# First batch on eight PSUM banks, early loads over two queues, first head group's q/k copied inside SBUF

## The chip, the cores and the metric

The kernel runs on one core of a Trainium2 chip. The metric is the device time of one execution in microseconds. Engines are named as in the profile: PE (TensorE), with PEld for its weight loads, DVE (VectorE), ACT (ScalarE), POOL (GpSimd) and SP (SyncE, which only issues DMAs). SPq and POOLq are their queues.

## The reference

Input x is (4, 512, 256), 4 batches of 512 tokens. All is fp32.

```
qh = heads((layernorm(x) @ wq + bq)) * gqw      # gqw, gkw: one weight per token
gq = sum over tokens of qh
gk = sum over tokens of (heads(ctx @ wk + bk) * gq * gkw)
out = heads(ctx @ wv + bv) * gk + qh
x1 = x + tanh(g_xattn) * (out @ wo + bo)
src = layernorm(x1)
attn = softmax(q k^T / 4) v  with q, k, v = src @ Wq + Bq, ... in 16 heads of 16
z = layernorm(src + attn @ Wo + Bo)
expert = floor(z @ router_w + router_b) mod 4
out = x1 + tanh(g_ffn) * layernorm(z + relu(z @ W1[expert] + b1) @ W2[expert] + b2)
```

## The kernel before

Each batch goes through the same stages. "x" are the layernorm statistics, "scale" normalises, cT and xT transpose ctx and x on PE, gv computes the gate vectors gq and gk from the token sums, Q and V are the gated projections, Y is the output projection; then "x1" (statistics), "src" (the second layernorm, L628), sT (its transpose), the projections q, k and v of the attention, and O after it. A task of PE such as q has two indices (halves of the features) and two halves (the two parts of the contraction).

The projections q and k are kept as a high and a low part for the fp32r products: ACT writes the high part (`HL[:, j, 0, :]`, L541), DVE the rest (L633). For a head group g the products need three pieces of q under each other (high, low, high) in QS and three of k (high, high, low) in KS, per half c of the heads. They get there through memory: `store_qk` (L291) writes HL to `qk_dram`, `load_stack` (L303, L306) reads twelve pieces of 16 partitions by two head pairs. A group has 16 row maxima (PE L818 into the three amax banks, DVE L686); they are negated, split and transposed, and go through `m_dram` (L312, L315) into rows 48 and 49 of QS, where the score product (L827, units u = 0 to 255) takes them up. ACT takes the exponentials (L549), PE multiplies by v (L839).

From u = -54 on all engines walk the same tables by unit (BLOCKS for PE, EVICT for ACT, VECTOR for DVE, QUEUE for SP, GPSIMD for POOL); batch b's entries are shifted by 64 b units, so batch 1's first part lies among batch 0's maxima, which run 24 units ahead of the scores. Each engine executes its list in order and waits on semaphores.

Batch 0 goes ahead of the tables, in the order of `LEAD` (L248). All side work uses two PSUM banks (`side`); the other six stand unused until the maxima start. SP's order ahead of the tables (L318 to L349) is: x and ctx of batch 0, the gates and gqw as a column, two rows broadcast to all partitions, five bias columns (element by element), eight broadcast rows, all weights, x and ctx of batch 1 (which wait for the first batch's x1 to be stored), and then the stores and stacks of batch 0. DVE computes twelve constants once all those loads have landed (L701 to L717), and PE's gv waits for all twelve. POOL computes the reciprocal roots (L396, L398), adds biases to xin (L413, L421), stores x1 (L423), adds a bias to src, stores it (L431) and reads it back into t_r (L437) after the store has landed; its list is in order as well.

## Time and profile before

| | us |
|---|---|
| median of 3 runs | 615.15 (612.97 to 615.59) |
| the profiled execution | 614.73 |
| its span | 612.9 |
| PE busy | 491.3 (80%) |
| DVE busy | 390.2 (64%) |
| ACT busy | 244.7 (40%) |
| POOL busy | 207.1 (34%) |
| mean granted TensorE clock | 0.858 of full |

Shares of the span are means over stages of different kinds. The first scores come at 112.2 us and the last at 417.3 us of the span; ahead of them lies the first batch's preparation, behind them the routed feed-forward.

### The profile page before, as it was taken

To read this page: it belongs to the slowest core of one execution; us is meant where nothing else is said; L and a number is where in the kernel's file an instruction comes from. 1 tells how busy PE (TensorE), PEld (TensorE's weight loads), DVE (VectorE), ACT (ScalarE), POOL (GpSimd) and SP (SyncE) were. 2 spreads that over 40 slices of the span, in tenths; PEclk is the share of its full clock that TensorE was granted. 3 is DMA by queue.
4 is the path that set the end of the run, shared out by engine and by line. 5 is a ranking of instruction groups with operands and counts; after the bars stand their busy time and mean duration, and the time that the engine had idled before them with its cause. 6 is when DMAs were issued, how large, how long until landed. Compare 5 with 4: busy or idle time off the path is not lost. (4 is left out here: it accounts for less than half of the span.)

```text
span 612.9 us, 8282 instructions
## 1 busy us (share of the span) xinstructions
PE 491.3 (80%) x2528; PEld 281.8 (46%) x2528; DVE 390.2 (64%) x871; ACT 244.7 (40%) x482; POOL 207.1 (34%) x273
## 2 busy tenths in 40 slices
PE   2095769899898999999979798887239998988970
PEld 2053343434423433434332242223239988888970
DVE  2333446988768889679976779703885655655552
ACT  2000200465435456244654546447005555454440
POOL 3115110141101323403303248522144565455552
PEclk9997957999789899799995879655659999899995
DMA  5701844055334353632665840020021122111220
GB/s 145 164 0 38 282 129 67 3 198 180 84 78 121 114 196 93 139 102 58 152 187 140 176 112 3 2 70 1 1 68 35 51 61 58 45 52 40 64 54 25
DMA packets 41795, 55.00 MB, mean 90 GB/s; under 512 B 14367, under 2 KB 26143, under 8 KB 41760
## 3 DMA queue, kind: packets, MB, share of 16 engines
q1 hardware_dynamic: 36432, 38.84, 24.3%
q0 software_dynamic: 5328, 15.74, 8.5%
q8 instruction: 16, 0.26, 0.2%
q14 instruction: 19, 0.16, 0.1%
HBM read 37.51 MB, written 17.83 MB: 90 GB/s over the span
## 5 line engine op out<-in xcount | busy, mean ns | idle before, releaser
L549 ACT ACTIVATE probs<-sc 128x512 f32<-128x512 f32 x256 | 141.2, 595 | 178.0 <-PE sc L827 175.5
L686 DVE TENSOR_REDUCE mx<-amax 128x1 f32<-128x512 f32 x256 | 166.6, 677 | 58.9 <-PE amax L818 58.8
L827 PE MATMUL sc<-QS,KS 50*128 50x512 f32 x256 | 111.7, 520 | 15.3 <-ACT probs L549 12.2
L818 PE MATMUL amax<-KS,QS 48*128 48x512 f32 x256 | 110.4, 515 | 14.4 <-DMA KS<-qk_dram 8.5
L827 PEld LDWEIGHTS sc<-QS,KS 50*128 50x128 f32 x256 | 45.6, 210 | 121.2 <-issue 64.9
L818 PEld LDWEIGHTS amax<-KS,QS 48*128 48x128 f32 x256 | 43.9, 205 | 32.0 <-DVE mx L686 15.2
L1174 PE MATMUL amax<-W_hi,hid_hi 128*128 128x256 f32 x160 | 48.2, 301 | 3.8 <-DVE hid_lo L1074 3.6
L1174 PE MATMUL amax<-W_hi,hid_lo 128*128 128x256 f32 x160 | 46.6, 291 | 0.0
L1174 PE MATMUL amax<-W_lo,hid_hi 128*128 128x256 f32 x160 | 46.6, 291 | 0.0
L495 POOL TENSOR_TENSOR an<-av,rec 128x256 f32<-128x256 f32 x16 | 10.2, 637 | 106.8 <-DVE rec L675 106.7
L839 PE MATMUL pv<-probs,V1b 128*32 128x512 f32 x256 | 44.1, 769 | 1.4 <-ACT probs L549 1.2
L396 POOL TENSOR_SCALAR var_eps<-mv 128x4 f32<-128x4 f32 x12 | 2.8, 235 | 120.5 <-DVE mv L571 116.1
L758 PE MATMUL side<-xcT,w_first 128*128 128x512 f32 x64 | 40.8, 760 | 0.0
L839 PE MATMUL pv<-probs,V1a 128*32 128x512 f32 x256 | 39.6, 695 | 0.0
L991 ACT ACTIVATE t_a<-sc,b_col 128x256 f32<-128x256 f32 x40 | 19.3, 482 | 42.6 <-PE sc L1164 42.4
L930 POOL DMA_INDIRECT out_dram<-slot_z,ids_now x22 | 24.2, 1099 | 35.4 <-DVE slot_z L1114 32.0
L758 PE MATMUL side<-srcT,w_second 128*128 128x512 f32 x64 | 34.6, 667 | 0.8 <-ACT srcT L535 0.8
L1174 PEld LDWEIGHTS amax<-W_hi,hid_hi 128*128 128x128 f32 x160 | 32.0, 200 | 6.2 <-DVE hid_lo L1074 6.0
L1164 PE MATMUL sc<-slot_xT,W_hi 128*128 128x256 f32 x160 | 31.5, 292 | 1.5 <-DVE slot_xT L1068 1.5
L1174 PEld LDWEIGHTS amax<-W_lo,hid_hi 128*128 128x128 f32 x160 | 32.1, 200 | 0.0
L1174 PEld LDWEIGHTS amax<-W_hi,hid_lo 128*128 128x128 f32 x160 | 32.0, 200 | 0.0
L1074 DVE TENSOR_TENSOR hid_lo<-t_a,hid_hi 128x512 fp32r<-128x512 f32 x40 | 27.0, 690 | 6.0 <-ACT hid_hi L992 5.7
(180 smaller groups left out, 865.8 us busy)
## 6 DMA issues: line engine op xcount, KB each, us to landing
qk_dram<-HL SPq DMA_DIRECT2D x16, 512.0 KB, 4.6
QS<-qk_dram SPq DMA_DIRECT2D x96, 64.0 KB, 2.9
KS<-qk_dram SPq DMA_DIRECT2D x96, 64.0 KB, 3.0
W_sb<-in_L_ffn_W SPq DMA_DIRECT2D x8, 512.0 KB, 5.5
xc<-in_x SPq DMA_DIRECT2D x4, 512.0 KB, 3.6
xc<-in_ctx SPq DMA_DIRECT2D x4, 512.0 KB, 4.8
x_dram<-xc POOLq DMA_DIRECT2D x4, 512.0 KB, 3.4
res_dram<-t_a POOLq DMA_DIRECT2D x4, 512.0 KB, 5.4
```

The source lines that it names most:

```text
L495: nc.gpsimd.tensor_tensor(an[:, :, g % 2, :], av_v[:, :, 0:DH], rec[:, :].unsqueeze(2).broadcast_to([P, S // 32, DH]), ALU.mult).then_inc( ...
L549: nc.scalar.activation(probs[:, n % 8, c * 512:(c + 1) * 512], sc[c][:, :], ACT.Exp, scale=SCALE).then_inc(exp_done, 1)
L686: nc.vector.reduce_max(mx[:, to:to + 1], amax[m % 3][:, :], AX.X).then_inc(max_done, 1)
L758: last = nc.tensor.matmul(bank[:, :], w[:, k, c * P:(c + 1) * P], src[:, k, :], start=(k == 0), stop=(k == KD - 1))
L818: nc.tensor.matmul(amax[m % 3][:, :], QS[rows, pair, chunk * P:(chunk + 1) * P], KS[rows, pair, :], start=True, stop=True).then_inc(A_full, 1)
L827: nc.tensor.matmul(sc[c][:, :], KS[rows, pair, kc * P:(kc + 1) * P], QS[rows, pair, :], start=True, stop=True).then_inc(sc_full, 1)
L839: last = nc.tensor.matmul(pv[32 * hh:32 * hh + 32, :], V1[b % 2][:, kc, 8 * c + pair, :], probs[:, (2 * r + hh // 2) % 8, c * 512:(c + 1) ...
L930: nc.gpsimd.indirect_dma_start(out_rows, bass.IndirectOffsetOnAxis(ap=ids_now[:, a:a + 1], axis=0), slot_z[:, a, :], None, bounds_check=NT ...
L991: nc.scalar.activation(hid[:, q % 2, f % 2, :], hid_bank[f % 4], ACT.Relu, bias=bias)
L1074: nc.vector.tensor_tensor(low, hid[:, q % 2, :, :], high.bitcast(fp32), ALU.subtract).then_inc(hid_split, 1)
L1164: last = nc.tensor.matmul(hid_bank[f % 4], w, slot_xT[:, xp, k, :], start=((k, (xp, wp)) == steps[0]), stop=((k, (xp, wp)) == steps[-1]))
L1174: last = nc.tensor.matmul(amax[a][:, 0:D], (hid_hi, hid_lo)[xp][:, f, a * P:(a + 1) * P], w, start=(f == 0 and (xp, wp) == PARTS[0]), stop ...
```

## The change

- Side work of batch 0 uses eight banks: `LEAD_BANK` gives each task its own, `bank_of` replaces `side_bank`. The order is cT, V0, xT, V1, gv, Q, Y, .... In all batches V's eviction (L612) now comes ahead of Q's (L607) and goes straight into oT; in later batches they change places in the tables.
- The two transposes of t_a wait tile by tile instead of for all four tiles.
- gqw and the five bias vectors are loaded as 14 rows of 128 by ACT's queue, transposed in one PE instruction ahead of everything and copied by ACT into `columns`. ACT's queue loads wv as well. On SP, x and ctx are followed by the two broadcast rows, wk, wq, wo, the gates, and the other rows and weights; each weight has its own semaphore.
- DVE's constants are in three parts: six ahead of the ctx sums, bo's row behind them, five between Q and Y. tanh moves on ACT behind xT. V1's fills move behind the second layernorm. POOL's x1 step waits until all of src is scaled.
- Three products whose result is not used stand on PE ahead of sT.
- For the first head group of batch 0, q and k go from HL to QS and KS by DMAs inside SBUF, 16 partitions each: SP issues q of the first pair, then x of batch 1, then k of both pairs; ACT issues q of the second pair. The stores to memory follow, for groups 1 to 3. ctx of batch 1 is loaded ahead of them.
- In later batches group 0's q half of the stack is asked for at -36 and its k half at -31; group 2's at -6 instead of -10.

The core of the diff (indented less):

```
 pv = psum("pv", [P, 512])
+BANKS = side + sc + amax + [pv]
...
-         -31: ("stack", 0), -22: ("stack", 1), -10: ("stack", 2), 2: ("stack", 3)}
+QUEUE = {-117: ("load", 0), -42: ("store", 0), -39: ("store", 1), -37: ("store", 2), -36: ("stack", (0, "q")), -34: ("store", 3),
+         -31: ("stack", (0, "k")), -22: ("stack", (1,)), -6: ("stack", (2,)), 2: ("stack", (3,))}
 QUEUE.update({16 * g - 8: ("maxima", g) for g in range(G)})
...
-FIRST_PART = [("cT", 0), ("cT", 1), ("xT", 0), ("xT", 1), ("gv", 0), ("Q", 0), ("V", 0), ("Q", 1), ("V", 1), ("Y", 0), ("Y", 1)]
-LEAD = FIRST_PART + [("sT", 0), ("sT", 1), ("q", 0), ("q", 1), ("k", 0), ("k", 1), ("v", 0), ("v", 1)]
+LEAD = [("cT", 0), ("cT", 1), ("V", 0), ("xT", 0), ("xT", 1), ("V", 1), ("gv", 0), ("Q", 0), ("Q", 1), ("Y", 0), ("Y", 1),
+        ("sT", 0), ("sT", 1), ("q", 0), ("q", 1), ("k", 0), ("k", 1), ("v", 0), ("v", 1)]
+LEAD_BANK = {"cT": (0, 1), "V": (4, 5), "xT": (2, 3), "gv": (6,), "Q": (7, 0), "Y": (1, 2),
...
-def side_bank(task, i):
-
-    return 1 if task in ("gv", "V") else 0 if task == "Q" else i % 2
+def bank_of(task, i, b):
+
+    if b == 0 and task in LEAD_BANK:
+        return LEAD_BANK[task][i]
+    return 1 if task in ("gv", "Q") else 0 if task == "V" else i % 2
...
+        for i, part in enumerate(((0, 1, 0), (0, 0, 1))[side_of == "k"]):
+            at = 64 * c + DH * i
+            sp.dma_start(to[at:at + DH, r, :].bitcast(fp32), HL[DH * r:DH * r + DH, c + 2 * (side_of == "k"), part, :].bitcast(fp32)).then_inc((stack_loaded[0], stack_rest)[r], 16)
+
     def load_stack(b, g, sides="qk"):
         if g == 0:
-            for j in range(2 if sides == "q" else 4):
+            for j in range(4)[2 * (sides == "k"):4 - 2 * (sides == "q")]:
                 sp.wait_ge(qk_stored[j], b * 16 + 16)
+        elif b == 0:
+            for j in range(4):
+                sp.wait_ge(qk_stored[j], 16)
         wait(sp, sc_full, (b - 1) * UNITS + 16 * (g + 1))
         for c in range(2):
...
-    load_batch(0)
-    sp.dma_start(gqw_col[:, :], gqw.rearrange("(t p) o -> p (t o)", p=P), allow_slow_non_contiguous=True).then_inc(gates_loaded, 16)
+    load_tokens(0)
+    load_context(0)
+    sp.dma_start(gkw_row[:, :], gkw.rearrange("s o -> (s o)").partition_broadcast(P)).then_inc(rows_s_loaded, 16)
+    sp.dma_start(t1[:, :], gqw.rearrange("s o -> (s o)").partition_broadcast(P)).then_inc(rows_s_loaded, 16)
+    load_weight("wk", wk, wk_loaded)
+    load_weight("wq", wq, wq_loaded)
+    load_weight("wo", wo, wo_loaded)
     sp.dma_start(gates[:, 0:1], g_xattn.partition_broadcast(P)).then_inc(gates_loaded, 16)
     sp.dma_start(gates[:, 1:2], g_ffn.partition_broadcast(P)).then_inc(gates_loaded, 16)
-    sp.dma_start(t1[:, :], gqw.rearrange("s o -> (s o)").partition_broadcast(P)).then_inc(w_loaded, 16)
-    sp.dma_start(gkw_row[:, :], gkw.rearrange("s o -> (s o)").partition_broadcast(P)).then_inc(w_loaded, 16)
-    for i, v in enumerate((bq, bk, bv, Bq, Bk)):
-        sp.dma_start(cols[:, i, :], v.rearrange("(k p) -> p k", p=P), allow_slow_non_contiguous=True).then_inc(w_loaded, 16)
-    for i, v in enumerate((bo, Bo, Bv, ln1_g, ln1_b, router_w.rearrange("d o -> (d o)"), ln2_g, ln2_b)):
-        sp.dma_start(rows_bc[:, i, :], v.partition_broadcast(P)).then_inc(w_loaded, 16)
-    sp.dma_start(rb_col[:, :], router_b.partition_broadcast(P)).then_inc(w_loaded, 16)
-    for n, ap in (("wq", wq), ("wk", wk), ("wv", wv), ("wo", wo)):
...
+    sp.dma_start(rb_col[:, :], router_b.partition_broadcast(P)).then_inc(rows_loaded, 16)
     for n, ap in (("Wq", Wq), ("Wk", Wk), ("Wv", Wv)):
         load_weight(n, ap, W_loaded)
...
                 sp.dma_start(w_sb["Wo"][r:r + DH, t, :], Wo[h * DH:(h + 1) * DH, :]).then_inc(W_loaded, 16)
-    load_batch(1)
-    for side_of, js in (("q", (0, 1)), ("k", (2, 3))):
-        for j in js:
-            store_qk(0, j)
-
-        sp.wait_ge(stack_ready, 1)
-        load_stack(0, 0, side_of)
+    load_context(1)
+    sp.wait_ge(lo_done, 1)
+    sp.wait_ge(stack_ready, 1)
+    load_parts("q", 0, 0)
+    sp.wait_ge(lo_done, 2)
+    load_parts("q", 1, 0)
+    load_tokens(1)
+    for r in range(2):
+        for c in range(2):
+            sp.wait_ge(lo_done, 3 + c)
+            load_parts("k", c, r)
+    for j in range(4):
+        store_qk(0, j)
     for g in range(1, G):
         load_stack(0, g)
...
-            pool.wait_ge(consts_ready, CONSTS)
+            pool.wait_ge(bo_ready, 1)
         for t in range(TT):
...
     def store_x1(b):
+        if b == 0:
+            pool.wait_ge(consts_ready, CONSTS)
...
 def act_program(act):
-    act.wait_ge(gates_loaded, 48)
-    nc.scalar.activation(tg[:, :], gates[:, :], ACT.Tanh).then_inc(gates_ready, 1)
+    for v, first in ((gqw.rearrange("s o -> (s o)"), 0), (bq, 4), (bk, 6), (bv, 8), (Bq, 10), (Bk, 12)):
+        n = v.shape[0] // P
+        act.dma_start(column_rows[first:first + n, :], v.rearrange("(k p) -> k p", p=P)).then_inc(columns_loaded, 16)
+    act.dma_start(w_sb["wv"][:, :, :], wv.rearrange("(k p) n -> p k n", p=P)).then_inc(wv_loaded, 16)
+    act.wait_ge(columns_full, 1)
+    nc.scalar.activation(columns[:, :], amax[2][:, 0:14], ACT.Identity).then_inc(columns_done, 1)
...
             wait(act, qk_stored[j], b * 16)
+            if b == 1:
+                act.wait_ge(stack_loaded[0], 12 * 16)
+                act.wait_ge(stack_rest, 6 * 16)
...
     for task, i in LEAD:
         side_work(task, i, 0)
+        if (task, i) == ("xT", 1):
+            act.wait_ge(gates_loaded, 32)
+            nc.scalar.activation(tg[:, :], gates[:, :], ACT.Tanh).then_inc(gates_ready, 1)
+    act.wait_ge(lo_done, 2)
+    act.wait_ge(stack_ready, 1)
+    for c in range(2):
+        for i, part in enumerate((0, 1, 0)):
+            row = 64 * c + DH * i
+            act.dma_start(QS[row:row + DH, 1, :].bitcast(fp32), HL[DH:2 * DH, c, part, :].bitcast(fp32)).then_inc(q_rest, 16)
...
             nc.vector.tensor_tensor(gkb[:, :], gk[:, :], cols[:, 2, :], ALU.mult).then_inc(gk_done, 1)
+        elif task == "V":
+
+            dve.wait_ge(V_full, b * 2 + i + 1)
+            dve.wait_ge(gk_done, b * 2 + 2)
+            wait(dve, Y_full, b * 2)
+            nc.vector.scalar_tensor_tensor(oT[:, i, :], bank[:, :], gk[:, i:i + 1], C1[:, i, :], ALU.mult, ALU.add).then_inc(t1_done, 1)
         elif task == "Q":
             dve.wait_ge(Q_full, b * 2 + i + 1)
-            dve.wait_ge(gk_done, b * 2 + 2)
-            wait(dve, csum_done, b * 2 + 2)
...
-
-            dve.wait_ge(V_full, b * 2 + i + 1)
...
-            nc.vector.scalar_tensor_tensor(oT[:, i, :], bank[:, :], gk[:, i:i + 1], t1[:, :], ALU.mult, ALU.add).then_inc(o_done, 1)
+            nc.vector.scalar_tensor_tensor(oT[:, i, :], bank[:, :], gkb[:, i:i + 1], oT[:, i, :], ALU.add, ALU.add).then_inc(o_done, 1)
...
             if i == 0:
-                dve.wait_ge(o_done, min(b + 3, B) * 2)
+                dve.wait_ge(csum_done, min(b + 3, B) * 2)
+                dve.wait_ge(consts_ready, CONSTS)
                 wait(dve, dot_done, b * (TT + 2))
...
         side_work("scale", t, 0)
-    dve.wait_ge(w_loaded, W_LOADS * 16)
-    dve.wait_ge(gates_ready, 1)
-
-    for row, g in ((BO, 0), (G2, 1), (B2, 1)):
-        nc.vector.tensor_scalar(rows_bc[:, row, :], rows_bc[:, row, :], tg[:, g:g + 1], None, ALU.mult).then_inc(consts_ready, 1)
+    dve.wait_ge(rows_s_loaded, 32)
+    dve.wait_ge(columns_done, 1)
...
-    nc.vector.tensor_tensor(rows_bc[:, GRW, :], rows_bc[:, G1, :], rows_bc[:, RW, :], ALU.mult).then_inc(consts_ready, 1)
-    dve.wait_ge(consts_ready, 8)
...
-                side_work("src", t, 0)
+
+    def later_constants():
+        dve.wait_ge(rows_loaded, 8 * 16)
+        for row in (G2, B2):
+            nc.vector.tensor_scalar(rows_bc[:, row, :], rows_bc[:, row, :], tg[:, 1:2], None, ALU.mult).then_inc(consts_ready, 1)
+        nc.vector.tensor_tensor(rows_bc[:, GRW, :], rows_bc[:, G1, :], rows_bc[:, RW, :], ALU.mult).then_inc(consts_ready, 1)
+        dve.wait_ge(consts_ready, EARLY_CONSTS + 3)
+        nc.vector.reduce_sum(gsum[:, 2:3], rows_bc[:, GRW, :], AX.X).then_inc(consts_ready, 1)
+        dve.wait_ge(csum_done, 2)
+        nc.vector.tensor_tensor_reduce(out=t1[:, 0:D], in0=rows_bc[:, B1, :], in1=rows_bc[:, RW, :], scale=1.0, scalar=rb_col[:, 0:1],
+                                       op0=ALU.mult, op1=ALU.add, accum_out=gsum[:, 3:4]).then_inc(consts_ready, 1)
+
+    side_work("cT", 0, 0)
+    side_work("cT", 1, 0)
+    dve.wait_ge(gates_ready, 1)
+    dve.wait_ge(bo_loaded, 16)
+    nc.vector.tensor_scalar(rows_bc[:, BO, :], rows_bc[:, BO, :], tg[:, 0:1], None, ALU.mult).then_inc(bo_ready, 1)
+    for task, i in (("gv", 0), ("V", 0), ("V", 1), ("Q", 0), ("Q", 1)):
+        side_work(task, i, 0)
+    later_constants()
+    side_work("Y", 0, 0)
+    for t in range(2):
+        side_work("x1", t, 0)
+    side_work("Y", 1, 0)
+    for t in range(2, TT + 1):
+        side_work("x1", t, 0)
+    for t in range(TT):
+        side_work("src", t, 0)
+    for v in V1:
+        nc.vector.memset(v[:, :, :, DH:2 * DH], 1.0).then_inc(v1_ready, 1)
+    for task, i in LEAD[LEAD.index(("q", 0)):]:
+        side_work(task, i, 0)
     for u in range(BEGIN, END + OVER):
         if 0 <= u + AHEAD < END:
...
-    def transposes(bank, src, c, full):
+    last_use = [None] * len(BANKS)
+
+    def transposes(bank, src, c, full, ready=None, b=0):
         for t in range(TT):
+            if ready is not None and c == 0:
...
             pe.wait_ge(stack_loaded[g % G], g // G * 192 + 192)
+        if m == 8:
+            pe.wait_ge(stack_rest, 6 * 16)
+            pe.wait_ge(q_rest, 6 * 16)
...
     pe.wait_ge(pool_ready, 3)
+    pe.wait_ge(columns_loaded, 6 * 16)
+    nc.tensor.transpose(amax[2][:, 0:14], column_rows, ident[0:14, 0:14]).then_inc(columns_full, 1)
     for task, i in LEAD:
-        if task == "gv":
-            pe.wait_ge(consts_ready, CONSTS)
+        for first, s, count in ((("V", 0), wv_loaded, 16), (("V", 0), cT_done, 2), (("gv", 0), wk_loaded, 16), (("gv", 0), wq_loaded, 16), (("Y", 0), wo_loaded, 16), (("sT", 0), W_loaded, W_LOADS2 * 16)):
+            if (task, i) == first:
+                pe.wait_ge(s, count)
+        if (task, i) == ("gv", 0):
+            pe.wait_ge(columns_done, 1)
         if (task, i) == ("sT", 0):
-            pe.wait_ge(W_loaded, W_LOADS2 * 16)
+            for _ in range(3):
+                nc.tensor.matmul(amax[2][:, :], w_sb["wq"][:, 0, 0:P], cT[:, 0, :], start=True, stop=True)
         for half in range(1 if task in ("cT", "xT", "gv", "sT") else 2):
             side_work(task, i, half, 0)
+    for n in range(len(side), len(BANKS)):
+        pe.wait_ge(*last_use[n])
     pe.wait_ge(stack_ready, 1)
     pe.wait_ge(v1_ready, 2)
...
```

## Rows read from the trace of the kernel before

**Rows 1.** Six stretches: length, busy time (and instructions) per engine, granted clock, DMA share, GB/s.
```profile
0.00:28.00 28.00, 3.88 (x16) 3.14 (x16) 6.59 (x22) 3.84 (x8) 5.67 (x11) 1.00 0.70 167
28.00:62.00 34.00, 23.11 (x62) 13.78 (x63) 13.22 (x31) 1.88 (x3) 12.41 (x16) 0.87 0.08 23
62.00:82.30 20.30, 11.24 (x40) 6.54 (x38) 7.46 (x18) 3.95 (x7) 5.00 (x8) 0.84 0.74 241
82.30:112.20 29.90, 28.36 (x74) 13.47 (x74) 20.39 (x39) 0.69 (x2) 0.00 (x0) 0.69 0.39 76
112.20:417.80 305.60, 280.87 (x1293) 109.22 (x1292) 231.13 (x492) 154.07 (x284) 91.05 (x116) 0.87 0.41 111
417.80:612.90 195.10, 143.82 (x1050) 135.67 (x1048) 111.39 (x271) 80.28 (x178) 92.95 (x122) 0.85 0.15 44
```

**Rows 2.** Timeline, 0 to 31 us: start, duration, engine, line, operation, count, [idle before <-releaser].
```profile
5.91 1.94 PE L753 MATMUL side<-ident,xc 128*128 128x128 f32 x8 [5.91 <-DMA xc<-in_ctx]
...
10.81 0.20 POOL L406 TENSOR_TENSOR rg<-rstd,gqw_col 128x4 f32<-128x4 f32 x1
...
24.54 0.88 DVE L705 TENSOR_SCALAR rows_bc<-rows_bc,tg 128x256 f32<-128x256 f32 x3 [12.11 <-DMA w_first<-in_L_xattn_wo]
...
29.72 0.98 DVE L591 CUSTOM_DVE_ANT_0 t<-xcT,gkw_row 128x512 f32<-128x512 f32 x1
```

**Rows 3.** Timeline, 30 to 62 us.
```profile
30.85 1.84 PE L790 MATMUL side<-xsum,w_first 128*128 128x1 f32 x8 [16.34 <-DVE csum L591]
...
34.26 9.57 PE L758 MATMUL side<-xcT,w_first 128*128 128x512 f32 x16
...
44.77 3.69 PE L766 MATMUL side<-w_first,oC 128*128 128x256 f32 x16 [0.94 <-DVE oC L612]
...
48.49 0.75 DVE L618 SCALAR_TENSOR_TENSOR xc<-side,tg,xc 128x512 f32<-128x512 f32 x1 [0.98 <-PE side L766]
...
52.45 2.19 DVE L628 TENSOR_SCALAR t_a<-xc,mv,rstd 128x256 f32<-128x256 f32 x4 [1.48 <-POOL rstd L398]
...
57.26 2.76 POOL L429 TENSOR_TENSOR t_a<-t_a,rows_bc 128x256 f32<-128x256 f32 x4
...
57.50 5.46 PE L758 MATMUL side<-srcT,w_second 128*128 128x512 f32 x6 [0.78 <-ACT srcT L535]
```

**Rows 4.** Timeline, 62 to 82.5 us.
```profile
62.02 0.75 DVE L633 SCALAR_TENSOR_TENSOR HL<-side,cols,HL 128x512 fp32r<-128x512 f32 x1 [7.38 <-ACT HL L541]
...
67.20 0.76 POOL L437 DMA_DIRECT2D t_r<-res_dram  x1 [6.06 <-DMA res_dram<-t_a]
...
76.81 1.08 PE L753 MATMUL side<-ident,t_a 128*128 128x128 f32 x4 [4.30 <-DVE t_a L585]
...
80.50 0.42 SPq L303 DMA_DIRECT2D QS<-qk_dram  x1
...
82.34 0.79 PE L818 MATMUL amax<-KS,QS 48*128 48x512 f32 x2 [4.45 <-DMA KS<-qk_dram]
```

**Rows 5.** Timeline, 97 to 116 us.
```profile
97.56 0.42 SPq L306 DMA_DIRECT2D KS<-qk_dram  x1
...
102.70 1.98 PE L758 MATMUL side<-xcT,w_first 128*128 128x512 f32 x4
...
105.14 0.67 SPq L312 DMA_DIRECT2D m_dram<-mT  x1
...
112.18 0.50 PE L827 MATMUL sc<-QS,KS 50*128 50x512 f32 x1
```

**Rows 6.** DMA issues, 0 to 100 us: KB each, median us from issue to landing.
```profile
qk_dram<-HL SPq DMA_DIRECT2D x4, 512.0 KB, 4.5
QS<-qk_dram SPq DMA_DIRECT2D x24, 64.0 KB, 2.9
...
gqw_col<-in_L_xattn_gqw SPq DMA_DIRECT2D x1, 2.0 KB, 4.5
...
w_first<-in_L_xattn_wv SPq DMA_DIRECT2D x1, 256.0 KB, 8.9
```

78 lines of the change are left out of this document (37 added, 41 removed), and 2 rows, old and new, of the table BLOCKS.

## The prediction

> **What bounds the kernel now.** I read the profile in three steps: the busy time cut by stretches, then the timeline of the first 116 us, then the landing times of the DMAs. The stretches [rows 1] show a kernel of three parts. From 112.2 to 417.8 us runs the attention loop (305.6 us, TensorE busy in 280.9 of them), from 417.8 to 612.9 the routed feed-forward, 195.1 us. The rest, 112.2 us, is the lead-in: batch 0 goes through its first part, its q/k/v and its first head group's maxima before the first score. In 0 to 28 us TensorE is busy for 3.9 us, DVE for 6.6. The loop and the tail start when the lead-in ends, and no line of the tail is touched, so nearly the whole question is by how much the first score, at 112.18 [rows 5], comes earlier.
>
> The lead-in is a chain with four links. (1) DVE's constants start at 24.54, released by the last weight load after 12.11 us of idling, and TensorE's first real block (gv) starts at 30.85 behind them [rows 2, 3]. (2) gv 3.7 us (twice 1.84), Q and V 9.57, Y 3.69, the second layernorm, and the q block starts at 57.50 [rows 3]. (3) The low half of q0 is done at 62.77, is stored and read back, and the first product for the maxima runs at 82.34, released by a DMA into KS [rows 4]. (4) The maxima, with batch 1's first part between them, take from 82.34 to 105.14, the way of the maxima through memory until the first score 7.04 more [rows 5].
>
> **The change, part by part.** I keep a clock for the new kernel and compare at each mark.
>
> *Loads.* SP issues x and ctx first as now. The ACT queue issues six loads of rows (14 rows of 128 numbers) and wv. Seven issues at about 0.47 (as the stack loads: 36 from 80.50 to 97.56 [rows 4, 5]) put wv out at some 4 us. Landing of the small ones is bounded by 2.9 us (a 64 KB stack load) and 4.5 us (gqw_col) [rows 6]: 7 to 8.5 us on the clock, I take 7. wv is bounded by 2.9 below and 8.9 above, its present landing behind the full queue [rows 6]: 7 to 13 us; the stretch 62 to 82.3 moves 241 GB/s against 167 in the first 28 [rows 1], so without the element-wise column loads ahead of it I take the lower half, under 10. The new wait of TensorE on the columns stands ahead of the ctx transposes, which now start at 5.91 [rows 2]: they slip to 7.3 (1.94 us, ACT's copies until 9.8), and everything of PE is queued behind. The rule of the Trainium skill that speaks against this part is in "DMA: Bandwidth & Descriptors", section "Issuing engines are not separate DMA queues": transfers started by scalar, sync or gpsimd run on the same 16 engines, and a second issuer saves only issue time. By it the second queue would be worth seven issues of 0.47, 3.3 us of SP's time, and no bandwidth. No row of before has an ACT-issued load, so it isn't shown here.
>
> *First part.* V0 runs as soon as ctx is transposed and wv is there: 9.9. Q and V took 9.57 for 16 records [rows 3], V0 as a quarter at the cold rate is 3.4 (5.46 for 6 records is 0.91 each, 1.98 for 4 is 0.5 [rows 3, 5]). The x transposes follow at 13.3 (x is scaled by then: rg is there at 10.81 even now [rows 2]), V1 to about 18.3, gv to 21 (3.7 cold, 2 warm; I take 2.7), Q0 and Q1 to 24.4 at the warm rate. DVE's constants for this part (two sums, two C1, two bG) lie beside V0 and the x transposes. Its csum pass needs 0.98 at most each [rows 2], done by 14. From gv on DVE does V0, V1, Q0, Q1 at 0.75 each; the last waits for Q1: o is done at 25.2. Y 3.69 on PE to 29.0, DVE's last Y step at 29.0, which is at 48.49 now [rows 3]: minus 19.5. The five later constants (some 2 us) stand between Q and Y on DVE, beside Y's first half (1.85); uncovered they cost 2. The eight banks remove the waits of V on Q's eviction; within Q and V these are small, as 16 records fill the 9.57 without a gap [rows 3]; I give them nothing.
>
> *Second layernorm to q.* From 48.49 to the scaling at 52.45 is 3.96 us, unchanged. The scaling takes 2.19 for four now because POOL adds beside it; the new wait on src_done takes POOL away, and the transposes follow tile by tile. I take 1.4 and 0.6 us of overlap. The wait delays POOL's four adds (2.76 as their like [rows 3]) by 1 us, for which only the store of x1 waits. DVE's two fills of V1, now beside gv, go behind the scaling, where DVE has nothing before q's low half. Three products on no one's data fill 6 records before sT: 2.6 us warm, done at 31.6, ahead of the first scaled tile at 32.9; cold they would end at 34.1 and cost 1. Their purpose can be priced from rows: the 6 cold records of q cost 5.46 where warm ones cost 3, and the stretch 28 to 62 has a mean granted clock of 0.87 [rows 1, 3]. The page "TensorE: Matmul & The Clock Gate", section "The HAM clock gate", of the Trainium skill says that the slow level is the default and activity releases it, so filling is the right cure; by it the gain is these 2.5 us. The q block starts at 35.4 instead of 57.50, q0's low half is done at 38.7 instead of 62.77: minus 24. At the warm rate (1.7 a task) k1's low half is done at 43.8 and v at 45.9.
>
> *First group without memory.* Now: store (4.5), wait, six loads, landing 2.9, for q and again for k [rows 6]. New: q pieces at 38.8 to 42, then x of batch 1, k pieces of the first pair until 45.3 (three issues of 0.47 for each half), landing 2.9: the stacks stand at 48.2. That is 34 us before 82.34. But I don't grant it all, for batch 1's x transpose is ahead of the first maxima in TensorE's order (76.81 and 82.34 now [rows 4]). POOL has to finish batch 0's residual: adds until 41.5, its store, and 6.06 us of waiting for it before it may reload [rows 4]: 48.3, then 0.76 for the issue, then batch 1's scale (1.48 from statistics to scaling [rows 3] and 0.20 for rg [rows 2], with the hand-over some 1.8), DVE's scaling 1.4, the transpose behind its first tile: 51 to 52.3. So the first maxima start at 52.0, bounded by 48.2 and by 54 (a slower reload): minus 30.3.
>
> *Maxima to first score.* Now 29.84 us from 82.34 to 112.18 [rows 4, 5], at a mean clock of 0.69, DVE busy 20.4 [rows 1]. At the same pace the first score comes at 81.9. At the full clock the stretch can't be shorter than DVE's 20.4; but another queue then binds. SP has the four stores (48.0 to 50), waits for their landing (4.5 alone, 6 for 2 MB together: 56), and issues 36 stack loads, 17.5 us [rows 4, 5]: 73.5. Only then does it take the first maxima, after which 7.04 us pass: 80.5. Both bounds are so close that I take 81.0: minus 31.2. The six ACT-issued pieces of the second pair lie in ACT's idle time (43 to 46 us; its next job is a copy at 47.5).
>
> *Loop.* Later batches change V and Q places (the same records), ask for three more landings long past, and issue q's half of the stack before k is stored: 6 issues less, 2.8 us, where PE waits for KS; between nothing and 2 us in each of two batches. The second group's loads move by four steps, still ahead of use. I take 0 and keep minus 4 in the range.
>
> Sum against the profiled execution, 614.73 us (span 612.9, 1.83 around it): 614.7 - 31.2 = 583.5. It lies 0.4 below the median of 615.15, which gives 584; for the many marks at which something may slip I go 1 up: 585.
>
> **The rivals.**
>
> *A: the early loads stay the limit* (0.2). For it: 4.7 MB come in by 28 us (167 GB/s times 28 [rows 1]), nearly all of it is still loaded, and wv, wk and wq share engines with two 256 KB broadcasts. Against: the low rate falls into the column loads. If weights land 6 us later than I think, gv starts at 24 and the gain is 25: 590; range 588 to 597.
>
> *B: the loop gains too* (0.17). The clock stays high between v and the maxima, q's earlier stack loads save 2 us a batch, and the loop's mean of 0.87 rises. Gain 36 to 42: 573 to 579. Against: SP's 36 loads bind at 80.5 whatever the clock.
>
> *C: the direct move does not reach the first product, or is slow* (0.08). A piece has 16 partitions with 2 KB each; if 18 of them take the 4.5 us of a 512 KB store one after the other, the first maxima start at 55 to 58 and the score at 86: 588 to 591. In its weak form the move does not do what it says because the x transpose at 50.9 is later than the stack; that is in my forecast.
>
> *D: slower than before* (0.02). The mechanism: loop and tail at a lower granted clock. The loop's 280.9 us of TensorE at 0.87 [rows 1] grow to 326 at 0.75, +45 against -31: 629. It decides from a mean of 0.78 on (280.9 x 0.87/0.78 = 313, +32). For it only that the clock is 0.69 in one stretch; against it that the loop's order is unchanged.
>
> **How the numbers follow.** Forecast with its own range 580 to 588: 0.53; A 0.2, B 0.17, C 0.08, D 0.02. The range 576 to 595 leaves out the end of B, the end of A and D, some 0.15. A change of less than 0.5% is about what a measurement of this kernel can't tell from none; only D and a failure of every part lie there or above. Faster 0.97, same 0.01, slower 0.02.
>
> **What would show it.** gv at 18 to 19 instead of 30.85; last Y step on DVE near 29; q block near 35.4 with a granted clock of 1.0; stacks landed before batch 1's x transpose, which is near 51 and releases the first maxima; SP issuing stack loads until about 73; first score at 80 to 82; loop 304 to 307 us and tail 195. It is wrong if the first maxima come before 48 or after 56, if the first score is not within 78 to 86, or if the loop's length moves by over 4 us.

## The result, and the profile after

| | before | after |
|---|---|---|
| median, us | 614.06 (609.24 to 615.59, 4 runs) | 583.08 (573.46 to 589.22, 4 runs) |
| the profiled execution | 614.73 | 580.17 |
| its span | 612.9 | 578.1 |
| first score / last score | 112.2 / 417.3 | 83.1 / 382.8 |

The ratio of the two medians is 0.950. A ratio with an interval, here 0.941 (0.928 to 0.954), counts for each kernel only the runs within 1.5% of its fastest, which leaves out the longer two of after's four (585.98 and 589.22); a kernel with only one such run is given none. In the last row stand three parts: the lead-in went from 112.2 to 83.1 us (-29.1), the loop from 305.1 to 299.7 (-5.4), the tail from 195.6 to 195.3.

The lead-in is the way to the first score, the loop lies between the first and the last score, and the tail behind them. The stretches after, cut at the first maxima and at the first score (length, busy us and instructions of PE, PEld, DVE, ACT, POOL, granted clock, DMA share, GB/s), against [rows 1]:

```profile
0.00:28.00 28.00, 18.06 (x67) 11.35 (x68) 14.85 (x40) 4.02 (x9) 8.44 (x15) 1.00 0.70 178
28.00:52.45 24.45, 16.46 (x57) 9.17 (x55) 11.93 (x31) 5.03 (x8) 11.24 (x17) 0.92 0.51 157
52.45:83.07 30.62, 28.98 (x74) 14.62 (x73) 20.61 (x39) 1.38 (x4) 2.85 (x4) 0.67 0.54 125
83.10:382.80 299.70, 274.77 (x1291) 107.82 (x1290) 232.00 (x491) 154.27 (x284) 91.14 (x116) 0.89 0.43 113
382.80:578.10 195.30, 144.21 (x1054) 135.78 (x1050) 111.56 (x271) 80.19 (x178) 93.76 (x122) 0.85 0.15 43
```

In its first 28 us PE works 18.1 instead of 3.9, with DMA at the same share (0.70) and much the same rate (178 against 167 GB/s). The DMA engines carry hardly more than before; what changed is which load stands first and who waits for which. The loop's row has 274.8 us of PE at 0.89 where it had 280.4 at 0.87.

Timeline of the first part (start, duration, engine, line, operation, count, idle before and its releaser), against [rows 2, 3]:

```profile
8.22 0.25 PE L910 MATMUL amax<-ident,probs 14*128 14x14 f32 x1 [8.22 <-DMA probs<-in_L_ffn_bk]
...
11.12 0.50 PEld L821 LDWEIGHTS amax<-xcT,w_first 128*128 128x128 f32 x2 [1.15 <-DMA w_first<-in_L_xattn_wv]
11.15 3.65 PE L821 MATMUL amax<-xcT,w_first 128*128 128x512 f32 x4 [0.78 <-ACT xcT L567]
...
12.85 0.69 DVE L641 CUSTOM_DVE_ANT_0 t<-xcT,gkw_row 128x512 f32<-128x512 f32 x1 [0.15 <-DVE bG L759]
...
17.23 0.95 PE L853 MATMUL amax<-xsum,w_first 128*128 128x1 f32 x8
...
27.28 0.75 DVE L667 SCALAR_TENSOR_TENSOR xc<-sc,tg,xc 128x512 f32<-128x512 f32 x1 [0.19 <-PE sc L829]
```

PE's first block waits for the columns (8.22; their rows lie in a buffer that the profile calls probs), V0's weight load for wv (1.15 us of idling), V0's first product for ACT's copy of the ctx transposes, done at 11.00. The two came close together: wv had landed at about 10.6 (issued at 2.85, 7.7 us to landing). gv starts at 17.23 instead of 30.85. Its two records take 0.95 and 1.03 us, and DVE's last Y step is at 27.28 instead of 48.49. A block is called warm below when its products run at the pace of a clock granted in full, and cold at the pace of half of it. V0 is cold by its own duration, four products in 3.65 us where V1's four take 1.88 (from 15.51), though the row of the first 28 us shows a granted clock of 1.00.

Two things had to be there for gv: the weights and the sums of the tokens. Before, wk was issued at 14.00 and took 8.6 us to land:

```profile
14.00 0.47 SPq L274 DMA_DIRECT2D w_first<-in_L_xattn_wk  x1
```

```profile
w_first<-in_L_xattn_wk SPq DMA_DIRECT2D x1, 256.0 KB, 8.6
```

So before's gv could not have started ahead of about 22.6 whatever DVE did (an estimate, 14.00 + 8.6). In fact it waited for DVE, which idled 12.11 us for the last of the loads, then computed constants from 24.54 on, and began its pass over ctx for the sums (csum, L591) only at 28.88. After, wk is issued at 2.82 and takes 8.1, and that pass (L641) starts at 12.85. By this estimate at least 5 of gv's 13.6 us come from wk landing earlier, that is from the order of the loads and from the columns that stood ahead of them, and at most 8 from the shorter waits for constants. No run parts the two. From here to the first maxima, against [rows 3, 4]:

```profile
33.74 3.67 PE L821 MATMUL amax<-srcT,w_second 128*128 128x512 f32 x8 [0.83 <-ACT srcT L570]
...
36.46 0.75 DVE L682 SCALAR_TENSOR_TENSOR HL<-amax,columns,HL 128x512 fp32r<-128x512 f32 x1 [2.22 <-ACT HL L580]
...
41.11 0.91 SPq L288 DMA_DIRECT2D xc<-in_x  x1
...
42.06 7.50 SPq L309 DMA_DIRECT2D KS<-HL  x12
...
43.58 0.76 POOL L469 DMA_DIRECT2D t_r<-res_dram  x1 [3.24 <-DMA res_dram<-t_a]
...
47.03 1.40 DVE L615 BATCH_NORM_STATS2 stats<-xc 128x6 f32<-128x256 f32 x4 [2.00 <-DMA xc<-in_x]
...
51.17 1.35 PE L816 MATMUL side<-ident,t_a 128*128 128x128 f32 x4 [5.42 <-DVE t_a L633]
...
52.45 0.79 PE L883 MATMUL amax<-KS,QS 48*128 48x512 f32 x2
```

The eight products of the q block take 3.67 us with the clock granted in full; six took 5.46 before. Batch 1's x is issued at 41.11 behind q's pieces, is in use at 47.03, and its scaled tile releases the transpose (51.17) right behind which the maxima start at 52.45, against 82.34. No wait for a KS piece is shown ahead of it. The end of the lead-in, against [rows 4, 5]:

```profile
73.92 0.42 SPq L327 DMA_DIRECT2D KS<-qk_dram  x1
74.39 0.67 SPq L333 DMA_DIRECT2D m_dram<-mT  x1
...
77.62 1.28 SPq L336 DMA_DIRECT2D QS<-m_dram  x2
...
79.53 3.61 PE L829 MATMUL side<-w_first,oC 128*128 128x256 f32 x8
...
83.07 0.49 PE L892 MATMUL sc<-QS,KS 50*128 50x512 f32 x1
```

And four DMA issues (KB each, median us from issue to landing), against [rows 6]:

```profile
KS<-HL SPq DMA_DIRECT2D x12, 32.0 KB, 3.9
...
w_first<-in_L_xattn_wv ACTq DMA_DIRECT2D x1, 256.0 KB, 7.7
...
QS<-HL SPq DMA_DIRECT2D x6, 32.0 KB, 2.0
QS<-HL ACTq DMA_DIRECT2D x6, 32.0 KB, 4.4
```

### The profile page after: what moved, and what is told of

It is laid out like the page before. It is cut to its first block and busy times, and to the rows that moved or that the text cites. A ratio compares the mean times of both kernels' runs of the same rounds, so it can differ in the third digit from the quotient of the medians.

```text
span 578.1 us, 8313 instructions
## 1 busy us (share of the span) xinstructions
PE 482.5 (83%) x2535; PEld 278.8 (48%) x2535; DVE 390.9 (68%) x871; ACT 244.9 (42%) x483; POOL 207.4 (36%) x273
## 5 line engine op out<-in xcount | busy, mean ns | idle before, releaser
L892 PE MATMUL sc<-QS,KS 50*128 50x512 f32 x256 | 108.1, 502 | 14.9 <-ACT probs L588 12.5
L883 PE MATMUL amax<-KS,QS 48*128 48x512 f32 x256 | 106.9, 500 | 11.0 <-DMA KS<-qk_dram 6.2
L892 PEld LDWEIGHTS sc<-QS,KS 50*128 50x128 f32 x256 | 43.7, 202 | 115.9 <-ACT probs L588 56.1
L883 PEld LDWEIGHTS amax<-KS,QS 48*128 48x128 f32 x256 | 42.0, 197 | 28.0 <-DVE mx L736 13.8
L904 PE MATMUL pv<-probs,V1a 128*32 128x512 f32 x256 | 35.4, 626 | 0.1
L821 PE MATMUL side<-xcT,w_first 128*128 128x512 f32 x52 | 31.6, 715 | 0.0
L722 DVE STREAM_TRANSPOSE av<-pv 128x512 f32<-128x512 f32 x16 | 11.3, 707 | 24.8 <-PE pv L904 24.8
```

What stands on the lines that cost most here:

```text
L821: last = nc.tensor.matmul(bank[:, :], w[:, k, c * P:(c + 1) * P], src[:, k, :], start=(k == 0), stop=(k == KD - 1))
L883: nc.tensor.matmul(amax[m % 3][:, :], QS[rows, pair, chunk * P:(chunk + 1) * P], KS[rows, pair, :], start=True, stop=True).then_inc(A_full, 1)
L892: nc.tensor.matmul(sc[c][:, :], KS[rows, pair, kc * P:(kc + 1) * P], QS[rows, pair, :], start=True, stop=True).then_inc(sc_full, 1)
L904: last = nc.tensor.matmul(pv[32 * hh:32 * hh + 32, :], V1[b % 2][:, kc, 8 * c + pair, :], probs[:, (2 * r + hh // 2) % 8, c * 512:(c + 1) ...
```

## The experiments

The kernels fall into three groups, each timed beside its own runs of the kernel before: a1 to a4 (before 606.1 us), a5 to b2 (614.1) and b3 to c2 (611.6). Times compare within a group, ratios across them. A kernel's time came from 2 runs in the first two groups and from 6 in the last, so times are told beside the marks of the one profiled execution: "first maxima" and "first score". After has 52.45 and 83.07; its own code, run again (c0), 52.35 and 82.06, so a difference of 1 us in a mark tells nothing by itself.

### Undoing one part at a time

**a1_through_memory.** The first group goes through memory again: all four stores, then its twelve loads. ACT's six pieces go too; the rest stays.

```diff
-            load_parts("q", 0, 0) ... load_parts("k", c, r)
+            store_qk(0, 0); store_qk(0, 1); load_tokens(1); store_qk(0, 2); store_qk(0, 3)
-            for g in range(1, G):
+            for g in range(0, G):
                 load_stack(0, g)
```

> The changed kernel, but its first head group goes through memory as before (all four stores, then the twelve loads of group 0); everything else as changed. Marks of the changed kernel: first product for the maxima 52.45, first score 83.07. Theory 1 (batch 1's x chain gates the first maxima, the copies inside SBUF save only a few us): stores out by 43, landed by 48, twelve loads issued until 54 and landed at 57: first maxima at 56 to 57, first score 3 to 5 us later than 83.07 (86 to 88), since SP is free of twelve slower issues. Rival 2 (the round trip is what the change gained, as in the kernel before, where 19.6 us lay between the first low half and the first maxima): first maxima at 62 or later, first score 91 or later.

585.7 us (581.2 to 590.2). Timeline of a1:

```profile
56.58 0.79 PE L867 MATMUL amax<-KS,QS 48*128 48x512 f32 x2 [6.05 <-DMA KS<-qk_dram]
...
76.78 0.67 SPq L333 DMA_DIRECT2D m_dram<-mT  x1
```

First maxima 56.58, now released by the DMA into KS after 6.05 us; first score 86.84. The direct move is worth 4.1 us at the maxima and 3.8 at the score, of the 30 us by which the first maxima come earlier. SP had issued all loads by then and took the maxima the moment they were there (76.55 + 0.21 to 76.78); the way from maxima to score was 30.3 all the same.

**a2_no_fill.** The three products ahead of sT are taken out.

```diff
-                if (task, i) == ("sT", 0):
-                    for _ in range(3):
-                        nc.tensor.matmul(amax[2][:, :], w_sb["wq"][:, 0, 0:P], cT[:, 0, :], start=True, stop=True)
```

> The changed kernel without the three products on no one's data. TensorE then idles from 27.2 to 31.3. Theory 1: the granted clock falls to 0.5 in that gap or soon after, the first transposes and records of q run at 0.85 us instead of 0.43, q's low half comes 2 to 2.6 us later than 37.21, the first maxima 1 to 2.5 us later than 52.45. Rival 2: a gap of 4 us leaves the clock as it is, all marks within 0.3 us.

582.6 us (578.0 to 587.2). Timeline of a2:

```profile
34.20 5.96 PE L821 MATMUL amax<-srcT,w_second 128*128 128x512 f32 x8 [0.78 <-ACT srcT L570]
```

Eight records in 5.96 us instead of 3.67: +2.3, as expected. The first maxima came at 55.32, 2.9 later where 1 to 2.5 were expected, and the first score at 86.2. But the same cold block came in a6, b1 and b2, which have the fill; a6, from its timeline, and its windows (granted clock in the third column from the right; the last row is a6's loop):

```profile
34.78 5.46 PE L821 MATMUL amax<-srcT,w_second 128*128 128x512 f32 x6 [0.83 <-ACT srcT L570]
```

```profile
34.00:36.00 2.00, 1.22 (x2) 0.73 (x3) 1.12 (x2) 0.64 (x2) 2.00 (x4) 0.50 0.00 0
86.20:392.00 305.80, 281.56 (x1293) 109.31 (x1292) 232.05 (x492) 154.05 (x284) 91.13 (x116) 0.87 0.41 111
```

Of the twelve profiles with the fill (of four products in c2), after's among them, nine began the q block warm and three cold. So 2 to 3 us is what a cold block costs; how much of it the fill prevents one execution without it can't say.

**a3_two_banks.** Batch 0 uses two banks again, and the order that goes with them.

```diff
-        LEAD = [... ("V", 0), ("xT", 0), ("xT", 1), ("V", 1), ("gv", 0), ("Q", 0), ("Q", 1), ...
+        LEAD = [... ("xT", 0), ("xT", 1), ("gv", 0), ("V", 0), ("Q", 0), ("V", 1), ("Q", 1), ...
-            if b == 0 and task in LEAD_BANK:
-                return LEAD_BANK[task][i]
```

> The changed kernel with the side work of batch 0 in the two side banks again; V ahead of gv is impossible with two, so the order is cT, xT, gv, V0, Q0, V1, Q1, Y. Loads, constants, fill and copies as changed. Theory 1 (my prediction gave the banks nothing, the order with V ahead some microseconds, since V fills the wait for the loads): gv starts at about 14.5 instead of 17.23 but V and Q follow it, Q ends at 26 instead of 22.6; with bank waits between q, k and v the q block comes 3 to 4 us late and k's last low half 5 us late; first score 4 to 5 us later than 83.07. Rival 2 (the banks are a large part of the gain): first score 8 us later or more. Rival 3: under 1 us.

582.7 us, ratio 0.963 (0.952 to 0.973). Timeline of a3:

```profile
14.08 1.76 PE L851 MATMUL side<-xsum,w_first 128*128 128x1 f32 x8 [2.79 <-DVE csum L639]
...
17.40 8.89 PE L819 MATMUL side<-xcT,w_first 128*128 128x512 f32 x16
...
27.23 3.69 PE L827 MATMUL side<-w_first,oC 128*128 128x256 f32 x16 [0.94 <-DVE oC L659]
```

gv runs earlier, but 8.9 us of V and Q stand behind it, so Y starts 3.7 later than after's 23.55; first maxima 55.59, first score 86.11. The q block starts at 37.42, again 3.7 later, so two banks add nothing between Y and q. Banks and order together are worth 3 to 4 us, and it is the order that shows: V behind gv. The banks' own part is that they allow this order.

**a4_one_queue.** The seven early loads of ACT's queue go to SP, behind x and ctx.

```diff
-                act.dma_start(column_rows[first:first + n, :], ...
-            act.dma_start(w_sb["wv"][:, :, :], ...
+                sp.dma_start(column_rows[first:first + n, :], ...
+            sp.dma_start(w_sb["wv"][:, :, :], ...
```

> The changed kernel with the seven loads of ACT's queue (six of rows, wv) issued by SP right behind x and ctx; nothing else differs. Theory 1 (issuers share the engines, a second queue saves issue time only): columns are transposed at 8.2 to 9.5 (now 8.22), V0 at 11 to 12.5 (now 11.15), the SP loads behind them come 3.3 us later, the last piece of Wo is landed near 30 instead of 27, which now is a limit ahead of sT by 0.2 us only: fill and sT 1 to 2.5 us later, first score 1 to 3 us later. Rival 2 (a queue of its own brings the rows past the bulk): columns not before 11, V0 not before 14, first score 3.5 us or more later. Rival 3: no difference.

577.5 us (576.7 to 578.4), ratio 0.954 (0.944 to 0.964). First maxima 50.80, first score 80.46, 2.6 earlier than after and 1.6 earlier than c0. Its two timeline marks:

```profile
3.72 0.39 SPq L344 DMA_DIRECT2D w_first<-in_L_xattn_wv  x1
...
10.11 3.75 PE L821 MATMUL amax<-xcT,w_first 128*128 128x512 f32 x4 [0.78 <-ACT xcT L567]
```

SP issues wv 0.9 later than ACT did (2.85), and V0 still starts 1.0 earlier, and 0.6 before c0's 10.72. On SP's queue, ahead of the broadcast rows, wv took 3.5 us to land; issued by ACT beside them it took 7.7 in after and 7.7 to 9.3 in the other profiles. The expected loss of 1 to 3 us did not come, and the second queue brought nothing here. This is the side of the Trainium skill's "DMA: Bandwidth & Descriptors", section "Issuing engines are not separate DMA queues": a second issuer takes issue time off the first and adds no bandwidth. The trace agrees: with ACT as a second issuer SP's wk was out at 2.82 instead of a4's 5.14, and in the first 28 us after and c0 moved 178 and 169 GB/s, a4 172.

**a5_element_columns.** The columns are loaded element by element, as before, but over ACT's queue and with their own semaphore.

```diff
-                act.dma_start(column_rows[first:first + n, :], v.rearrange("(k p) -> k p", p=P)) ...
+                act.dma_start(cols[:, i, :], v.rearrange("(k p) -> p k", p=P), allow_slow_non_contiguous=True) ...
```

> The changed kernel with the column constants loaded element by element, as before, from ACT's queue ahead of wv, and no transpose by TensorE; everything else as changed. Theory 1 (the element-wise loads choke the DMA engines, in the kernel before 1,792 pieces of 4 bytes stood in front of the weights): wv lands 4 us or more later than 11.1 (V0 at 15 or later), the last weight likewise, and the first score comes 3 to 8 us later than 83.07. Rival 2 (with a semaphore for each weight the element loads hurt no one, the early constants were late only since they waited for all): all marks within 1 us, V0 perhaps earlier as TensorE has one wait less.

584.3 us, ratio 0.952 (0.935 to 0.969). Timeline of a5:

```profile
13.85 3.78 PE L820 MATMUL amax<-xcT,w_first 128*128 128x512 f32 x4 [4.83 <-DMA w_first<-in_L_xattn_wv]
...
20.43 0.95 PE L852 MATMUL amax<-xsum,w_first 128*128 128x1 f32 x8
```

V0 waits 4.83 us for wv and starts 2.7 later than in after; gv is 3.2 later, first maxima 55.76 and first score 86.63 (+3.6). The direction is theory 1's, the size less than its 4 us for wv: the element loads hold up what stands behind them, but account for about a quarter of the 13.6 us that gv gained. They run on a queue of their own here, so what they cost in before, where they stood in SP's queue, may differ. With them back, gv at 20.43 is still 10.4 us ahead of before's.

**a6_old_table.** In later batches the queue's old entries.

```diff
-                 -36: ("stack", (0, "q")), -34: ("store", 3), -31: ("stack", (0, "k")), -22: ("stack", (1,)), -6: ("stack", (2,)),
+                 -34: ("store", 3), -31: ("stack", (0,)), -22: ("stack", (1,)), -10: ("stack", (2,)),
```

> The changed kernel with SP's table for the later batches as before (the stack of group 0 in one piece at -31, group 2 at -10). The lead-in is untouched: first score 83.07 within 0.5. The loop takes 301.5 us in the profile of the changed kernel and 305.6 in that of before. Theory 1: the table makes nothing that can be told from the spread of the granted clock; the waits of the maxima for KS grow by up to 2.8 us in each of three batches at most, the loop is 300 to 306. Rival 2: the table is what shortened the loop, it is 305 to 307, and the waits of the maxima for KS come back to the 8.5 us of before from 6.2.

586.3 us, ratio 0.955 (0.946 to 0.964). Its loop took 305.8 us, 6.1 more than after's. Yet PE's waits for KS in it came to 3.8 us against 6.2 in after and 4.1 in before's loop (the 8.5 of the expectation includes the first group's wait ahead of it). The table's own mechanism did not show, and the loop's row, shown with a2, has a clock of 0.87 against 0.89.

### What holds the first score

Three kernels take away the suspects that the prediction named: SP's queue ahead of batch 1's x, SP's 36 loads ahead of the maxima, and the clock.

**b1_x_act.** ACT's queue loads batch 1's x as soon as src is scaled and x1 is stored.

```diff
-            load_tokens(1)
+                if (task, i) == ("k", 0):
+                    act.wait_ge(x1_stored, 16)
+                    act.wait_ge(src_done, TT)
+                    act.dma_start(xin[:, :, :], x[1, :, :] ...).then_inc(x_loaded, 16)
```

> The changed kernel with x of batch 1 issued by ACT behind k0's high half instead of by SP behind q's pieces. In the changed kernel it is issued at 41.11 and lands at 47.03, and it releases the statistics that lead to the first maxima at 52.45. Theory 1 (x's chain gates the first maxima): it lands 0.7 to 2 us earlier and the first maxima come as much earlier; the first score comes 0 to 1.5 us earlier, as SP's stack loads hold the first maxima's way until 74.4. Rival 2 (POOL's reload of the residual or the pieces gate it): first maxima within 0.3 us of 52.45.

580.2 us (575.3 to 585.1). Its q block was cold, so marks are counted from DVE's step for q0's low half (39.43): 15.0 us to the first maxima, where after has 16.0, c0 15.5, and the cold a6 16.8 and b2 18.1. c1 and c2 below carry the same edit (and four products ahead of the transpose) with a warm q block and have 14.1 and 14.0, where after, c0, b3, a4 and a5 have 14.8 to 16.1. A gain of 0.5 to 3 us at the maxima; the score comes at 85.42, 31.0 behind them.

**b2_maxima_first.** SP moves the first maxima after the loads of one group instead of three.

```diff
-            for g in range(1, G):
-                load_stack(0, g)
+            load_stack(0, 1)
+            move_maxima(0, 0)
+            load_stack(0, 2)
+            load_stack(0, 3)
```

> The changed kernel with SP moving the first group's maxima of batch 0 between the stack loads of group 1 and group 2 instead of behind group 3. In the changed kernel the maxima are ready at 72.9 and SP takes them at 74.39. Theory 1 (SP's loads bind by 1.5 us): they are taken at 73.0, the first score comes 1 to 2 us earlier than 83.07, unless TensorE's Y block of batch 1 (76.8 to 83.1, at half clock) stands in front of it: then 0. Rival 2 (SP is not a limit): 0; rival 3 (groups 2 and 3 come too late): the maxima of group 2 wait for KS and the loop grows by 2 us or more.

581.6 us, ratio 0.947 (0.935 to 0.960). First maxima 57.63, first score 88.54: 30.9 us between, as with the loads ahead. SP's loads don't hold the score here.

**b3_fill_gap.** Five products on no one's data stand ahead of batch 1's x transposes, in the gap in which the clock falls.

```diff
+                    if b == 1 and i == 0:
+                        for _ in range(5):
+                            nc.tensor.matmul(amax[2][:, :], w_sb["Wq"][:, 0, 0:P], srcT[:, 0, :], start=True, stop=True)
```

> The changed kernel with five more products on no one's data, ahead of batch 1's x transpose, where TensorE idles for 5.4 us (45.75 to 51.17) and the clock falls. In all nine profiles of the changed kernel and its variants the way from the first maxima to the first score took 29.7 to 31.0 us, with SP early or late, and 12 us or more of it at half clock. Theory 1 (half clock sets it): the first maxima come at the same time, the clock stays at 1.0 there, and the way shrinks to 22 to 26 us; first score 4 to 7 us earlier than in the run of the unchanged code beside it, unless SP's stack loads then hold the maxima (taken at 74.4 at the earliest, first score not before 80). Rival 2 (DVE or the order sets it): 29.5 to 31 as ever. Rival 3 (the clock falls all the same).

576.8 us (574.9 to 580.4), ratio 0.948 (0.943 to 0.953). The clock held until about 56 us instead of 48, then fell, and fell again at 76. First maxima 52.13, first score 83.18: 31.1 us between, no gain. The test is a weak one, as the mean clock of this stretch rose only from 0.67 to 0.73. The time is 4.1 us under c0's of the same group, with overlapping intervals; in the two profiles the difference lies in the loop (295.7 us against 301.4), not ahead of it.

**c0_changed_again, c1_x_act_fill_maxima, c2_x_act_more_fill.** c0 is the changed kernel. c1 joins b1, b2 and four products of b3's. c2 joins b1, four products of b3's and a fourth one ahead of sT, and leaves SP's order as it was.

> The changed kernel once more, word for word. The profiles so far differ in the granted clock although the code ahead of the difference is the same: the q block began warm at 33.7 in one and cold at 34.8 in two others, and the loop took 295 to 306 us, shorter where its mean clock was higher. Theory 1 (the clock differs from run to run): first score 81 to 87, loop 295 to 306 with its length following the mean granted clock, times over 573 to 590. Rival 2 (the loop's 299.7 us is a property of the change and the 305.8 of the run with the old table another): first score 83.1 and loop 299.7, each within 1 us.

> Three edits together on the changed kernel: x of batch 1 issued by ACT, four products of filling ahead of batch 1's x transpose, and the first maxima moved by SP ahead of the stack of group 2. Theory 1: first maxima 1 to 2 us earlier, the way to the first score 22 to 25 us as SP no longer holds them: first score at 73 to 77, the whole 6 to 9 us faster than the changed kernel. Rival 2 (SP is no limit even then): as the next kernel. Rival 3 (groups 2 and 3 arrive too late once PE is fast): the loop grows by 2 us or more for its clock.

> The changed kernel with x of batch 1 issued by ACT, four products of filling ahead of batch 1's x transpose, and four instead of three ahead of sT; SP's order of stacks and maxima as changed. Theory 1: the q block is warm more often, the maxima stretch warm as in the run with filling alone, but SP takes the first maxima only at its last stack load (73 to 74.5): first score at 78 to 81, 2 to 4 us behind the kernel with the maxima moved ahead. Rival 2 (SP is no limit): level with it or better.

Before was 611.6 (11 runs). c0: 580.9 (579.2 to 584.9), ratio 0.954 (0.949 to 0.959). c1: 573.4 (570.8 to 583.7), ratio 0.939 (0.933 to 0.945). c2: 577.8 (572.0 to 580.3), ratio 0.947 (0.941 to 0.953). c1 is the fastest version here, 7.5 us under c0. Timeline of c1:

```profile
50.92 0.50 PE L892 MATMUL amax<-KS,QS 48*128 48x512 f32 x2
...
70.74 0.67 SPq L333 DMA_DIRECT2D m_dram<-mT  x1
...
72.79 1.70 SPq L336 DMA_DIRECT2D QS<-m_dram  x2
...
73.88 0.79 PE L892 MATMUL amax<-KS,QS 48*128 48x512 f32 x1 [0.76 <-DVE mx L742]
...
74.60 2.07 PE L835 MATMUL side<-w_first,oC 128*128 128x256 f32 x4
...
77.33 3.56 PE L835 MATMUL side<-w_first,oC 128*128 128x256 f32 x8
...
80.81 0.50 PE L901 MATMUL sc<-QS,KS 50*128 50x512 f32 x1
```

The maxima leave at 70.74, the moment they are ready, yet the score is at 80.81 and not at the 73 to 77 expected. The rows name the reason: between the maxima's load (72.79) and the first score stand three maxima products and twelve records of batch 1's Y in TensorE's own list, 6.9 us from 73.88 to 80.81.

In c2 SP takes the maxima at 75.28, behind its loads, and there the score did wait for them:

```profile
81.58 0.50 PE L898 MATMUL sc<-QS,KS 50*128 50x512 f32 x1 [0.41 <-DMA QS<-m_dram]
```

It is the only one of the fourteen profiles in which the maxima's way through memory ends last, by 0.41 us. The two ways lie close together: after's maxima were loaded at 77.62 and, if they took c2's 2.7 us, were in place near 80.4 (an estimate), 2.7 us ahead of the score. The granted clock of that time, in c1:

```profile
52.00:54.00 2.00, 1.04 (x4) 0.49 (x3) 2.00 (x5) 0.69 (x2) 1.57 (x2) 1.00 1.02 377
58.00:60.00 2.00, 2.00 (x11) 2.00 (x11) 0.00 (x0) 0.00 (x0) 0.00 (x0) 0.50 0.44 106
72.00:74.00 2.00, 1.15 (x4) 0.49 (x3) 2.00 (x4) 0.00 (x0) 0.00 (x0) 0.92 0.05 8
76.00:78.00 2.00, 2.00 (x6) 0.87 (x5) 0.57 (x1) 0.00 (x0) 0.00 (x0) 0.50 0.54 140
80.80:375.90 295.10, 269.07 (x1291) 106.45 (x1290) 232.13 (x491) 154.17 (x284) 91.08 (x116) 0.92 0.45 118
```

It is 0.50, the lower of the two levels (1.2 of 2.4 GHz), in 76 to 78, behind a stretch in which PE was busy 1.15 of 2 us because it waited for DVE's reductions (in 72 to 74); a like sequence stands at 52 to 60. The four products put off the first fall and did not keep the clock up where DVE sets the pace.

c1's lead-in is only 1.3 us shorter than c0's. The rest is the loop, 295.1 us against 301.4:

```profile
82.10:383.50 301.40, 273.77 (x1293) 107.88 (x1292) 232.21 (x492) 154.24 (x284) 91.02 (x116) 0.89 0.43 112
```

The loops of the fourteen profiles mostly go with their clock: at 0.87 305.1 (before), 305.8 (a6) and 303.6 (b1); at 0.88 and 0.89 297.9 to 301.4, and 305.1 once (a5); from 0.90 on 295.0 to 295.7, and 298.8 once (a3). DVE works 228 to 232 us in every one. The four shortest are c1, c2, b3 (products in the gap) and a2 (no fill at all), which have no edit in common; whether the products ahead of the loop act on its clock stays open.

## Why the prediction was right

Predicted 585.0 us, 576 to 595; measured 583.1. The lead-in's links came in the order and nearly at the times forecast, but the cause of one was misread, and part of the nearness is luck. The four runs spread over 16 us, and from profile to profile 583.5 was forecast and 580.2 came: the lead-in gave 29.1 us instead of 31.2, loop and tail together 5.7 where nothing was forecast. By its own steps:

- **Loads.** Columns at 7 and wv under 10 put V0 at 9.9; it was 11.15. Right within 1.3 us; the columns came 1.2 later than taken (8.22), and with them the ctx transposes and their copies, while wv landed at about 10.6, not under 10. The second queue had no part in it (a4). The wait that ended, 12.11 us on DVE, was for the rows, the columns and the first four weights up to wo, not for all weights and batch 1's x, as the text ahead of the prediction has it: those of the attention were still being issued until 28.4.
- **First part.** V1 and gv were priced between warm and cold. All of V1 and gv was warm (gv 2.0 us instead of 2.7), and the last Y step came at 27.28, not 29.0. "I give them nothing", said of the eight banks as a cure for bank waits, agrees with a3, whose V and Q run without a gap in two banks. But the order that the prediction counts with, V ahead of gv, needs the banks, and a3 puts both together at 3 to 4 us: V moves into time in which TensorE had waited for the token sums. The prediction gave this part no price of its own.
- **To q.** q0's low half done at 37.21 against 38.7 (62.77 before): 1.5 early, by the early Y step. The fill's 2.5 us for a cold block is what a2 and a6 show (2.3 and more), but that the fill secures it isn't shown.
- **First group.** The first maxima at 52.45, predicted 52.0, by the link that the prediction put in front: batch 1's x transpose, not the stacks. Its cause was misread, though. POOL's reload waited 3.24 us, not 6.06, and was issued at 43.58, not 48.3. The gate is batch 1's x, issued by SP at 41.11 behind six pieces that take 0.63 each (7.50 us for twelve, not 0.47 each) and in use at 47.03. Two errors of opposite sign cancelled.
- **Maxima to first score.** Predicted 29.0, measured 30.6. SP took the maxima 1.5 us after they were ready, at 74.39, close to the bound of 73.5. But it did not bind: where SP was free (a1, b2, c1) the way stayed at 29.9 to 30.9, and only c2's score waited for the maxima, 0.41 us. The way is 29.7 to 31.1 us in all fourteen profiles, at clocks from 0.67 to 0.78. What stands in front of the score in the other thirteen is TensorE's list, whose last part runs at half clock behind DVE's pace; how much of the way is the clock's and how much DVE's isn't shown.
- **Loop.** "I take 0": 5.4 us came in the profile (rival B's sign, and past the 4 us that I had called the limit; by its own sign the prediction is wrong here). The same code gave 301.4 in c0, and the lengths mostly go with the clock, which this study can't tie to the table. That the clock came out higher because of the change isn't excluded: before's one profile is at 0.87, and five of the thirteen profiles with the change at 0.90 or more. Over whole executions of the last group it was 0.844 to 0.876 in before's eleven runs and 0.863 to 0.886 in c0's six, whose share of stages differs.
- **Rivals.** A (590) would have had gv at 24; it was at 17.23. C (maxima at 55 to 58) was not reached: pieces issued from 42.06 to 49.56 were there in time. B's loop came, its lead-in didn't. D fell with the clock at 0.89.

By links, the lead-in's 29.1 us are 13.6 up to gv, 7.6 from there to the last Y step, 4.4 from it to q0's low half, 4.3 from there to the first maxima and -0.8 to the first score. Undoing single parts gives 3.8 (direct move), 3 (banks and order), 3.6 (columns), some 3 (a warm q block) and -1.6 to -2.6 (second queue): about 11 of the 29.1 us, if the parts add up. Most of the rest lies ahead of gv. a5 and a3 show that it is neither the columns nor the banks: with the old columns gv still starts 10.4 us ahead of before's, with two banks and V behind it 16.8. What is left there is each load with its own semaphore, short waits for early constants and the loads' order. That group is shown by the marks; which of the three it is was not run. Open too is what a kept clock in the last 30 us would give.

## What to carry to other kernels

Ask first what an in-order engine waits for and whether it needs all of it: loads in the order of use, a semaphore for each and constants in parts moved gv by 10 us or more here, the direct transfer the first maxima by 4. Before you credit a faster transfer, read what stands ahead of its user in that engine's list: here it was batch 1's transpose at 51.17. Repeat the unchanged code before you explain a difference of some microseconds: marks of a timeline tell a part's worth where the total can't.
